# A fused attention, Gelu and mixture-of-experts kernel: the Gelu stage and the expert stage written as one program, without the barriers between them, with shared memory and with the first step's expert fixed

## The reference

```python
inter = gelu(x @ fi_w + fi_b)                    # 256 -> 1024
y     = layernorm(inter @ fo_w + fo_b + x) * fo_g + fo_be
x     = x_in + tanh(g_xattn) * y
h     = rms_weight * rms_normed(layernorm(x))    # what the experts see
top2  = the 2 largest of h @ gate_w.T (8 experts), softmax shares of the two
out   = x + tanh(g_ffn) * (layernorm(x) + sum over the 2 experts of
        share * (silu(h @ w1[e].T) * (h @ w3[e].T)) @ w2[e].T)   # 256 -> 896 -> 256
```

## Time and profile before

| what | value |
|---|---|
| median of 3 runs | 2051.25 us |
| the profiled execution | 2046.32 us |
| its span, first to last instruction | 2044.6 us |
| granted TensorE clock, mean | 0.930 |
| TensorE busy (matmul) | 1812.3 us, 89% |
| VectorE busy | 1461.2 us, 71% |
| ScalarE busy | 1222.3 us, 60% |
| GpSimd busy | 1172.0 us, 57% |

### The profile page before, as it was taken

One profiled execution on the slowest core, in us unless ns is written; L12 is line 12 of the kernel. 1 busy time (PEld: TensorE's weight loads), 2 busy tenths in 40 slices (PEclk: granted clock), 3 DMA queues, 4 the chain that ended last, 5 costly groups with the idle time before them and its releaser, 6 DMA issues. The chain is left out here.

```text
span 2044.6 us, 36356 instructions
## 1 busy us (share of the span) xinstructions
PE 1812.3 (89%) x12326; PEld 1336.8 (65%) x12326; DVE 1461.2 (71%) x2914; ACT 1222.3 (60%) x2305; POOL 1172.0 (57%) x989
## 2 busy tenths in 40 slices
PE   0799799999999999998994999960999999999996
PEld 0455355554555555554542888850999999999996
DVE  5378688888888888786881588882777676676772
ACT  0166576666767667665673554530777777777773
POOL 6533464445646445543335546661687787877875
PEclk8599899999999999998997999975999999999998
DMA  2664455655556656446412222124667667676662
GB/s 90 115 132 97 96 106 110 131 117 115 110 110 110 131 115 120 97 88 118 95 33 75 57 83 92 70 84 142 225 210 235 216 213 221 213 230 220 210 225 39
DMA packets 117005, 270.61 MB, mean 132 GB/s; under 512 B 15802, under 2 KB 49722, under 8 KB 116436
## 3 DMA queue, kind: packets, MB, share of 16 engines
q1 hardware_dynamic: 102516, 249.57, 45.9%
q0 software_dynamic: 14304, 18.72, 4.6%
HBM read 196.50 MB, written 71.73 MB: 131 GB/s over the span
## 5 line engine op out<-in xcount | busy, mean ns | idle before, releaser
L703 DVE TENSOR_REDUCE nraw<-ps 128x1 f32<-128x512 f32 x1024 | 649.4, 684 | 201.7 <-PE ps L850 199.5
L618 ACT ACTIVATE spare<-ps 128x512 f32<-128x512 f32 x1024 | 571.4, 600 | 325.0 <-PE ps L860 320.5
L1748 POOL TENSOR_TENSOR u_lo<-u_f,u_hi 128x256 fp32r<-128x256 f32 x273 | 377.7, 1398 | 145.2 <-ACT u_hi L1782 145.2
L1854 PE MATMUL ps_e<-x_hi,we_hi 128*128 128x256 f32 x1092 | 313.0, 287 | 4.9 <-DVE we_lo L1668 4.9
L1854 PE MATMUL ps_e<-x_lo,we_hi 128*128 128x256 f32 x1092 | 305.9, 280 | 0.0
L1854 PE MATMUL ps_e<-x_hi,we_lo 128*128 128x256 f32 x1092 | 305.9, 280 | 0.0
L850 PE MATMUL ps<-kst,qst 50*128 50x512 f32 x1024 | 273.9, 446 | 36.1 <-DVE nraw L703 32.5
L860 PEld LDWEIGHTS ps<-qst,kst 52*128 52x128 f32 x1024 | 102.5, 186 | 282.7 <-ACT spare L618 189.1
L872 PE MATMUL ps<-spare,vaug 128*32 128x512 f32 x2048 | 279.4, 618 | 0.0
L860 PE MATMUL ps<-qst,kst 52*128 52x512 f32 x1024 | 270.6, 505 | 3.5 <-ACT spare L618 3.2
L1708 DVE TENSOR_TENSOR u_f<-ps_e,silu 128x256 f32<-128x256 f32 x273 | 115.1, 422 | 182.0 <-ACT silu L1813 180.8
(11 more groups left out here) (224 smaller groups left out, 3716.8 us busy)
## 6 DMA issues: line engine op xcount, KB each, us to landing
we_raw<-in_experts_w SPq DMA_DIRECT2D x117, 896.0 KB, 4.9
parts_kept<-parts SPq DMA_DIRECT2D x64, 512.0 KB, 3.3
kst<-parts_kept SPq DMA_DIRECT2D x192, 128.0 KB, 4.8
qst<-parts_kept SPq DMA_DIRECT2D x192, 128.0 KB, 5.9
x_raw<-xs SPq DMA_DIRECT2D x39, 259.0 KB, 2.8
x<-sum_tok SPq DMA_DIRECT2D x16, 512.0 KB, 2.6
x_tok<-x SPq DMA_DIRECT2D x16, 512.0 KB, 3.7
x_tok<-in_x SPq DMA_DIRECT2D x8, 512.0 KB, 4.5
```

Source lines behind the costliest of these rows:

```text
L618: act.activation(probs[:, e % 8], ps[:, score_bank(e, par)], ACT.Exp, scale=SCALE).then_inc(exp_made, 1)
L703: dve.tensor_reduce(nraw[:, g % 2, qt, half, i:i + 1], ps[:, max_bank(m, par)], AX.X, ALU.max, negate=True).then_inc(max_made, 1)
L1748: pool.tensor_tensor(u_lo[:, it], u_f[:, q % UPS], u_hi[:, it].bitcast(F32), ALU.subtract).then_inc(ulo_made, 1)
L1854: ins = pe.matmul(ps[:, q % UPS, c * GR:(c + 1) * GR], left, right, start=m == 0, stop=m == len(terms) - 1)
```

## The change

Both phases become `gelu_and_expert_phase`. The expert code is now a set of functions (`expert_programs`) that the Gelu stage's engine programs call at chosen places, in one block. The barrier at the end of the Gelu stage and the one after the small block are gone; waits on semaphores stand in for them. The tiles of both stages live in the same memory: the Gelu stage's weights and halves lie in the two buffers of `we_hi` and `we_lo`, its `gelu_out` in `we_raw`, and the expert stage's `x_raw`, `silu`, `u_f` and `eo` in the tile `spare`. The number of steps stays 39. Step 0 always belongs to expert 0, which gets at least one step:

```diff
+        step(dve.tensor_scalar(need[:, 0:1], need[:, 0:1], 1.0, None, ALU.max))
```

The functions that the Gelu stage calls:

```diff
+    def constants(pool):
+        pool.memset(zeros[:, :, :], 0.0).then_inc(consts_made, 1)
+        pool.wait_ge(consts_made, 1)
+        pool.iota(zeros[:, :, ROW], pattern=[[P, GT]], base=T, channel_multiplier=1,
...
+        pool.iota(steps_f[:, :], pattern=[[1, STEPS]], base=0, channel_multiplier=0,
...
+    def pad_once(sp):
+        sp.wait_ge(consts_made, 3)
+        sp.dma_start(scratch["xs"][NE * CAP:NE * CAP + GR, :].rearrange("(t p) d -> p t d", p=P),
+                     zeros[:, :, :]).then_inc(padded_once, 16)
+        sp.dma_start(scratch["out"][T:T + GR, :].rearrange("(t p) d -> p t d", p=P),
+                     zeros[:, :, 0:D]).then_inc(padded_once, 16)
+    def pad(sp):
+        sp.wait_ge(counts_made, 1)
+        for e in range(NE):
+            at = sp.value_load(counts_i[0:1, e:e + 1], min_val=0, max_val=T)
+            sp.dma_start(scratch["xs"][bass.ds(at + e * CAP, GR), :]
+                         .rearrange("(t p) d -> p t d", p=P), zeros[:, :, :]).then_inc(padded, 16)
+    def first_weights(sp):
+        sp.wait_ge(done["fo_done"], B * QT)
+        for c in range(3):
+            sp.dma_start(w_raw[:, c], A["experts_w"][0, c]).then_inc(raw_in[c], 16)
+    def first_high(act, c):
+        act.wait_ge(raw_in[c], 16)
+        act.activation(w_hi[:, 0, c], w_raw[:, c], ACT.Copy).then_inc(whi_made, 1)
+    def first_low(dve, c):
+        dve.wait_ge(whi_made, c + 1)
+        dve.tensor_tensor(w_lo[:, 0, c], w_raw[:, c], w_hi[:, 0, c].bitcast(F32), ALU.subtract)
```

Where they are called, and the waits before the first row load and the first products:

```diff
@@ sync @@
             load_x2(2)
+            then["pad_once"](sp)
             for i in range(2, B + 2):
...
+                if i == B + 1:
+                    then["first_weights"](sp)
                 store(i - 2)
...
-            sp.wait_ge(stored, 16 * B)
+            then["pad"](sp)
+            then["sync"](sp)
@@ gpsimd @@
+            then["constants"](pool)
             pool.wait_ge(fo_hi_made, 1)
...
-            for k in range(2):
-                pool.wait_ge(scattered[k], scatters(B - 2 + k))
+            then["gpsimd"](pool)
@@ scalar, period @@
+                    if s == 3 and i >= B:
+                        for c in ((0, 1) if i == B else (2,)):
+                            then["first_high"](act, c)
@@ vector @@
+                        if i == B + 1:
+                            then["first_low"](dve, 0)
...
             run(dve, period)
+            then["step_table"](dve)
+            for c in (1, 2):
+                then["first_low"](dve, c)
+            then["vector"](dve)
@@ sync of the experts, before the first row load @@
             if n == 0:
+                for s in range(2):
+                    sp.wait_ge(done["scattered"][s], done["all_scattered"])
+                sp.wait_ge(padded, 16 * NE)
+                sp.wait_ge(padded_once, 32)
@@ gpsimd and tensor of the experts @@
+        pool.wait_ge(done["stored"], 16 * B)
+        pool.wait_ge(padded_once, 32)
...
+        pe.wait_ge(done["gelu_made"], B * KF)
+        pe.wait_ge(done["sum_made"], B * QT)
+        pe.wait_ge(done["slots_made"], B)
```

More of the change, by code:

```diff
@@ L2 @@
 from concourse import mybir
+import math
 from contextlib import ExitStack
@@ L924, in gelu_phase, with gelu_and_expert_phase @@
+def gelu_and_expert_phase(nc, ctx, A, scratch):
     sb = lambda name, shape, dt=F32: ctx.enter_context(nc.sbuf_tensor(name, shape, dt))
@@ L927, in gelu_phase, with lent @@
     experts, running, first_row = A["experts"], A["running"], A["first_row"]
[L928 to L931, removed]
+    done = {}
+    E, then = expert_programs(nc, ctx, A, scratch, done)
+    def lent(tile, at, shape):
+        flat = tile.rearrange("p c n -> p (c n)")
+        cols = math.prod(shape)
+        if len(shape) == 1:
+            return flat[:, at:at + cols]
+        if len(shape) == 2:
+            return flat[:, at:at + cols].rearrange("p (a b) -> p a b", b=shape[1])
+        return flat[:, at:at + cols].rearrange("p (a b c) -> p a b c", b=shape[1], c=shape[2])
+    hi_0, hi_1, lo_0, lo_1 = (E[n][:, k] for n in ("w_hi", "w_lo") for k in range(2))
+    fi_hi, fi_lo = (lent(hi_1, n * KD * F, (KD, F)) for n in range(2))
+    fo_hi, fo_lo = (lent(lo_1, n * KF * D, (KF, D)) for n in range(2))
     gate_hi = sb("gate_hi", [P, KD, NE], F32R)
@@ L945, in gelu_phase @@
     x_tok = sb("gx_tok", [P, 2, QT, D])
-    s_tok = sb("s_tok", [P, QT, D])
+    s_tok = E["eo"].rearrange("p a t d -> p (a t) d")
     hn_tok = sb("hn_tok", [P, 2, QT, DX])
-    a_hi = sb("g_hi", [P, 2, KD, S], F32R)
-    a_lo = sb("g_lo", [P, 2, KD, S], F32R)
-    hn_hi = sb("hn_hi", [P, KD, S], F32R)
+    a_hi, a_lo = (lent(hi_0, n * 2 * KD * S, (2, KD, S)) for n in range(2))
+    hn_hi = lent(lo_1, 2 * KF * D, (KD, S))
     hn_lo = sb("hn_lo", [P, KD, S], F32R)
-    gelu_out = sb("gelu_out", [P, 4, S])
-    in_hi = sb("gelu_hi", [P, 4, S], F32R)
-    in_lo = sb("gelu_lo", [P, 4, S], F32R)
+    gelu_out = lent(E["w_raw"][:, :, :], 0, (4, S))
+    in_hi, in_lo = (lent(lo_0, n * 4 * S, (4, S)) for n in range(2))
     stats = sb("g_stats", [P, 2, QT, 6])
@@ L972, in gelu_phase @@
     slot_now = sb("slot_now", [P, 2, 2 * QT], U32)
-    ps = ctx.enter_context(nc.psum_tensor("ps_g", [P, 8, S], F32))
+    ps = E["ps"]
     FI, FO = 0, 2
@@ L1004, in gelu_phase @@
     scattered = [sem("scattered0"), sem("scattered1")]
+    done.update(fo_done=fo_done, gelu_made=gelu_made, sum_made=sum_made, slots_made=slots_made,
+                stored=stored, scattered=scattered, all_scattered=16 * 2 * QT * B // 2)
     n_rows = 5 + len(GELU_ROWS)
@@ L1203, in _ @@
             run(act, period)
+            then["scalar"](act)
         @block.vector
@@ L1893, in build @@
+            then["tensor"](pe)
 def build(nc, A, out):
@@ L1925, in build @@
         with ExitStack() as phase:
-            gelu_phase(nc, phase, A, scratch)
-        with ExitStack() as phase:
-            expert_phase(nc, phase, A, scratch)
+            gelu_and_expert_phase(nc, phase, A, scratch)
 def kernel(**inputs):
```

674 lines of the change are left out of this document (327 added, 347 removed).

## The result

| | before | the change |
|---|---|---|
| median of 4 runs each | 2051.59 us | 2037.87 us (2036.06 to 2040.05) |
| ratio, 95% interval | | 0.9934 [0.9917, 0.9951] |
| profiled execution, its span | 2046.32, 2044.6 us | 2037.22, 2035.5 us |
| granted clock, mean | 0.930 | 0.942 |
| TensorE busy | 89% | 1827.3 us, 90% |

The change is faster by 13.7 us, and the forecast was 28.4 us, with a range from 2018.6 to 2029.0 us. The sign was right, the size wrong.

What follows compares the result with a forecast made beforehand. TensorE was taken to bound everything from early in step 0, so starting it earlier gains as much. Terms -22.4 + 0.8 - 3.7 - 3.1 = -28.4 us, from 2051.25 to 2022.8 us; range 2018.6 to 2029.0.

Steps and rivals of the forecast that it cites:

- The loop of the steps: Expert stage's loop: same instructions and waits, shared memory adds none, so cost 0.
- Rival E: Expert loop loses pace through slower `u_lo` on GpSimd; 0.7 us more each gives 2089 us; chance 0.03.
- The issue of the row load: Between the stages: first row load issued at about 1398.35 instead of 1420.79, -22.4 us.
- padding and scatters at once: Between the stages: DMA shares 0.26 and 0.69 sum to just under full; charged 0.8 us, bounds 0 to about 2.
- The rule weighed: Scatters on GpSimd beside VectorE's table and two low parts: indirect DMAs still take 0.96 us, nothing charged.
- rival B: VectorE holds up the scatters, at most 3.97 us: gain -24.4 us, total 2026.8 us; chance 0.12.
- The row load's landing: Before step 0: no weights ahead in the queue, so median 2.8 us instead of 6.46, -3.7 us.
- The weights: Before step 0: weights ready early, so TensorE's wait for their low part goes, -3.1 us.
- rival D: Loads not early enough: weights 5 us late gives 2027.8 us, slow row load 2026.5; chance 0.10 for both parts.
- The clock: Start of step 0: slow products for 6.5 us at the lower clock, no difference taken.
- rival C: Step 0's slow-clock stretch vanishes or grows: 2019.5 or 2024.3 us; chance 0.10.
- The start of the Gelu stage: GpSimd's memset and iotas ahead of `fo_lo` have 7 us of cover: cost 0, some 1 us without it.

Runs made afterwards that it cites:

- e14_best: Changed kernel with one unused 64-byte tile behind the weight tiles, so x and u lie 64 bytes higher, over several executions; 2023.86 us, ratio 0.9877.
- e4_wait: Changed kernel with VectorE's second and third subtractions for step 0's weights held back until all scatters have landed; 2039.69 us.
- e18_pads_wait: e14_best with odd experts' zeros on ScalarE's queue and VectorE's second and third subtractions held until all scatters landed; 2022.02 us, ratio 0.9862.
- e2_shift32: Changed kernel with all tiles TensorE reads in the loop moved up by 32 bytes, their distances kept; 15.42 us a step, 2031.53 us.
- e8_before: Kernel before the change with its weight, x and u tiles moved to the changed kernel's addresses; 15.41 us a step, 2065.30 us.
- e1_addr: Changed kernel with the weight, x and u tiles put back on the addresses of the kernel before; 15.07 us a step, 2028.93 us.
- e9_off192: Changed kernel with one unused 64-byte tile behind the weight tiles, x and u 64 bytes higher, first run; 15.11 us a step, 2026.71 us.

## Why the prediction was wrong, step by step

**The loop of the steps: the step that failed.** "*The loop of the steps* has the same instructions and waits; shared memory adds none. ... Cost 0." It cost 12.2 us, 0.33 us on each of 38 steps. Instructions and waits were indeed the same and TensorE stayed busy; the matmuls themselves came 0.119 us apart on average instead of 0.114 and 0.118 in alternating slices. Rival E had the symptom (a step over 15.1 us), but named GpSimd's `u_lo` as the cause. In the changed kernel's trace its 242 subtractions between 1470 and 2000 us take 1393 ns each, in that of before 247 take 1414, so GpSimd was not slower. "Nothing in the trace shows a time that depends on a tile's place" is true of the place, but something in the trace asked for a reason and got none: equal slices of products took 1.42 and 1.37 us in turn, at a full clock and without a wait. A pace that changes with the work unchanged is a sign that something unnamed sets it. I had taken 546/36.2 as one number and never looked inside.

This can be seen by the starts of the slices. Timeline of TensorE in the changed kernel, the first matmul of each group of 12 (L1285) and of 6 (L1301):

```profile
1700.27 0.28 PE L1285 MATMUL ps_e<-x_hi,we_hi 128*128 128x256 f32 x1
...
1701.70 0.28 PE L1301 MATMUL ps_e<-we_hi,u_hi 128*128 128x256 f32 x1
...
1702.41 0.28 PE L1285 MATMUL ps_e<-x_hi,we_hi 128*128 128x256 f32 x1
...
1703.84 0.28 PE L1301 MATMUL ps_e<-we_hi,u_hi 128*128 128x256 f32 x1
```

and in e14_best (L1286, L1302):

```profile
1699.95 0.28 PE L1286 MATMUL ps_e<-x_hi,we_hi 128*128 128x256 f32 x1
...
1701.33 0.28 PE L1302 MATMUL ps_e<-we_hi,u_hi 128*128 128x256 f32 x1
...
1702.01 0.28 PE L1286 MATMUL ps_e<-x_hi,we_hi 128*128 128x256 f32 x1
...
1703.42 0.28 PE L1302 MATMUL ps_e<-we_hi,u_hi 128*128 128x256 f32 x1
...
1704.13 0.28 PE L1286 MATMUL ps_e<-x_hi,we_hi 128*128 128x256 f32 x1
```

1.43 + 0.71 each time in the first; 1.38 + 0.68, then 1.41 + 0.71 in the second.

**The issue of the row load and "padding and scatters at once": mis-sized.** Forecast, 13.5 us from `slot_now` to the row load's issue (1398.35 + 0.8 - 1385.65); measured, 15.8 (1406.01 - 1390.19). The term for running both at once was 0.8 us, from "0.26 and 0.69 ... Their sum is 0.95, just under full"; it came out at 3.1 us (15.8 less 1398.35 - 1385.65). The two shares are averages over stretches in which the engines also stood idle between bursts. At once they gave a share of 1.00 for 11 us, and each transfer took longer: about 9.9 us of the engines apart, 11.9 together. Adding the amounts of before would not have shown that either. The zeros landed after 2.6 to 4.9 us instead of 2.6 to 3.7, the last of them 14.9 us after `slot_now`, so about 2.2 us of the 3.1 would have come from the padding alone. (The "eight pieces" that the prediction counts in this number are seven; nothing is worked out from it.)

**The rule weighed, and rival B: the row was misread, the mechanism is real, its price nearly nil.** "So I charge nothing" rested on one indirect DMA beside subtractions of 128x512. That DMA had begun 0.11 us before the subtractions. One that began while such a subtraction ran stands in the same trace of before:

```profile
1266.75 0.69 DVE L1220 TENSOR_TENSOR gelu_lo<-gelu_out,gelu_hi 128x512 fp32r<-128x512 f32 x1 [2.12 <-ACT gelu_hi L1193]
1267.04 1.24 POOL L1095 DMA_INDIRECT xs<-hn_tok,slot_now  x1 [0.30 <-issue]
```

It ended at 1268.28, 0.84 us after the subtraction. The changed kernel shows the same with longer ones:

```profile
1397.22 3.95 DVE L1025 TENSOR_TENSOR we_lo<-we_raw,we_hi 128x1792 fp32r<-128x1792 f32 x2
```

The DMA that began at 1400.37 ended at 1402.00, 0.83 us after the second subtraction (1401.17), and the one that began at 1397.38 ended at 1400.06, again 0.83 us after the first (half of 3.95 us in, at 1399.2). So an indirect DMA that began inside such a subtraction was done only some 0.83 us after the end of it, where it takes 0.96 us alone. The two took 2.68 and 1.63 us, 2.4 us too much together, and without the subtractions 0.96 (e4_wait). The table beside them did not do this: during it the issues stayed at 0.96 to 1.03. The Trainium skill, SBUF — State Buffer, section "Who interferes with whom", counts a VectorE operation with two SBUF inputs among those that contend with GpSimd's reads, but infers that such a `tensor_tensor` does not hold up the writing of DMA descriptors. Here it held up the indirect DMAs as a whole; whether by the reading of their slots or by the writing of descriptors no run tells. But the zeros had landed only 0.7 us ahead of the last scatter, so at most that much was to be had: e4_wait and e18_pads_wait gained nothing without it. The 4 us that rival B charged assumed that the scatters alone decide.

**Right.** The row load's landing: 2.75 us against 2.8. The weights: ready, no wait for them between the turns and the last product of step 0's first slices; the first two high parts at 1367.55 and 1370.40, ahead of `hn_hi` at 1377.65 (rival D did not happen). From the rows' landing to the first product 3.06 us against 2.95. The clock: slow products for 6.0 us (1411.82 to 1417.81) against 6.5 (rival C did not happen). The start of the Gelu stage: the first matrix product comes 3.4 us after TensorE's first instruction in both kernels.

**The base of the forecast.** The gap between the span's difference (9.1) and the medians' (13.7) lies mostly in the attention phase, which took 6.0 us more in the change's profile. e2_shift32, with the changed code, began its Gelu stage at 1123.11, e8_before, with the code of before, at 1130.81.

## What to carry to other kernels

When memory is laid out anew, the pace of a loop that is bound by TensorE has to be priced like an added instruction: here 64 unused bytes a partition were worth 12 us, almost half of what the whole fusion brings in e14_best. Look inside the busy stretch first (equal groups of matmuls at unequal times), and try a few offsets between stationary and moving tiles. Where transfers that ran one after the other are to run at once, the sum of their shares in two windows is no forecast: here they filled the engines and took about a fifth more of their time than apart. And where a row shows two instructions side by side, look which of them began first before taking it as proof that they don't disturb each other.

## What the runs showed that I had not expected

The time from one 128x256 product to the next follows the distance, modulo 256 bytes, between the tile that is loaded as weights and the tile that streams: 0.120 us a product at distance 0 (two layouts 256 bytes apart both ran 4436 matmuls in 530 us), 0.119 at 128, and, with x and u both at 64 or 192, 0.114 and 0.118 in alternating slices. (In `up` the weights are loaded and x streams; in `down` u is loaded and the weights stream.) I found no part of the other engines in it: in the kernel before the mean time from product to product was 0.116 us beside `we_lo` on VectorE, beside `we_hi` on ScalarE, beside `u_lo` on GpSimd and while VectorE stood idle (worked out from the starts of some 2430 products between 1500 and 1800 us). That is not proof: at no product were all three idle, and in e14_best, where the fast and slow slices fall on the same places of every step, it was 0.117 beside `we_lo` and 0.116 without. The Trainium skill (the same section) gives TensorE two read ports of its own, one for the moving operand and one for weights, independent of each other, and says that TensorE waits on nobody. That fits with the kernel before, where the other engines made no difference. That the two reads are independent of each other is not what these layouts look like.

What stays open: why the distance counts at all (that the two reads meet somewhere is my reading of it, which no run shows), why the good layouts alternate between a fast and a slow slice (a fast slice takes 2.05 us and a slow one 2.13, so with all seven fast a step would be some 15.08 - 3.5 x 0.08 = 14.8 us, an estimate), why layouts with equal distances still differ by up to 0.04 us a step (e1_addr 15.07, e9_off192 15.11), and the distances 32 and 160, and weights or u at 0 apart from x, which weren't tried. The attention phase's spread of 8 us was seen, not explained.
